# Flamingo block: side jobs of layer 1's attention reordered with two staging buffers, and layer 0's tokens scaled and shifted as rows

## The chip, the cores and the metric

The kernel runs on one core of one Trainium2 chip. The metric is the time of one execution on the device, in microseconds (us). The core has five engines that run side by side, each through its own queue in order: TensorE (PE in the profile, its weight loads PEld), VectorE (DVE), ScalarE (ACT), GpSimd (POOL) and SyncE (SP, which here issues most DMAs). They wait for each other on semaphores.

## The reference, cut to what matters

```python
x = x + tanh(g_xattn[0]) * L0_xattn(ctx_1024, layernorm(x), ...)   # 8 batches, 512 + 512 keys, 8 heads of 128
x = x + tanh(g_ffn[0])   * L0_ffn(layernorm(x))                    # 16 experts, one for each token
x = x + tanh(g_xattn[1]) * L1_xattn(layernorm(x), ctx_1024)        # 16 heads of 16
x = x + tanh(g_ffn[1])   * L1_ffn(layernorm(x))                    # 8 experts, two for each token, and a shared one

def L0_xattn(x, latents, ...):
    xn = (x - mean) * rsqrt(var + eps) * gamma_media + beta_media       # the context's 512 tokens
    ln = (latents - mean) * rsqrt(var + eps) * gamma_lat + beta_lat     # the 512 tokens of x
    q = ln @ Wq + bq ;  k, v = split(concat([xn, ln]) @ Wkv + bkv)
    return softmax(q k^T / sqrt(128)) v @ Wo + bo                       # of each head
```

All is float32. A product is made of three products in a 32-bit format of TensorE (high times high, low times high, high times low), so each operand is kept as a high part, which ScalarE rounds out of PSUM, and a low part, which VectorE makes as value minus high part.

## The kernel before, in words

**Layer 0's attention** (tiles named `a_`) goes through 64 steps, `n = 8 b + 2 hp + par`: batch `b`, and head `2 hp + par`. Below a step is written (hp, par). A step has four row tiles of scores. `plan` writes out its order by hand: `scores0..3` are the products of query and key, `turn0..3` the transposes of the probabilities (`a_probT`), `fin0/1` the two halves of the product of probabilities and values of the head before, `out0/1` that head's output projection, `qk0..2` the queries and keys of the next head, and `v0..3` the values of two heads (in steps with par 0). All that isn't scores or transposes of probabilities goes through two PSUM banks, `a_pj`, in turn: use u may start when VectorE has emptied use u-2 (`free_bank`, semaphore `pj_out`). Step (3, 1) also has `pro2 pro3 pro0 pro1`: the four transposes of the next batch's normalised tokens `a_y`. ScalarE's part of a pro applies gamma and beta by column (`a_cols`) as it writes `a_kvT_hi`; VectorE applies them to PSUM in place (L457, `TENSOR_SCALAR a_pj`), and then writes `a_kvT_lo` (L437). `a_kvT` holds two batches. PE starts `scores2` when the exponential of `scores0` is done (`exp_done`), and so on.

`normalise` (L524) makes `a_y` of tokens, mean and inverse deviation on VectorE, a `TENSOR_SCALAR` for each of 8 tiles: all 8 in the opening, and for the next batch two tiles each at two places in step (2, 1) and two in step (3, 0). GpSimd splits the weights of each head in `split_w` (L304 to L308) and computes the inverse deviations in `inverse_std` (L315 to L325).

**The opening of layer 0** loads 13 constants first (semaphore `loaded`), the two big weights into `a_prob` among them, then the tokens (`x_load`) and the first heads' weights. ScalarE and VectorE split the big weights, PE sums the values' bias (L718, 8 products), then come normalise, the four pro and three qk, and step 0.

**Layer 1's attention** (tiles named `c_`) has 64 steps too, 8 pairs of heads in 8 batches; its scores begin at L2057. Ahead of each pair a row maximum is needed (`for_maximum` on PE L2046, `maximum` on VectorE L1831, 4 for each pair, AHEAD = 4 pairs). Before step 0 the opening must do for batch 0 and batch 1: turn the context (`ctx`) and the normalised tokens (`y`), project keys and queries (`k`, `q`), values (`v`), 16 maxima, and `max 0`, their transpose. These side jobs go through two banks of `c_side`, whose turn is the list `names`. A projected k or q is written by ScalarE and VectorE (`project_high`, `project_low`) into **one** staging tile `c_stage`; SyncE's `keep` writes it to DRAM in 4 DMAs, and `set_rows` reads it back as `c_q_rows`, `c_k_rows` in four quarters. So the next project_high waits until the last keep has landed (`staged`). GpSimd's `add_experts` adds the experts' rows to x when the x loads (`x_load`, 16 for each) are in; VectorE's `measure` takes the statistics; `normalise` follows on ScalarE.

Of the kernel before, what the change touches and what calls it, by code (L numbers as in the profile page):

```python
# [10 lines left out]
ALU = mybir.AluOpType  # L11
# [45 lines left out]
def layer0_attention(nc, t_in, K, tg, route, x1_dram, tables, qk_dram):  # L57
# [11 lines left out]
    with ExitStack() as ctx:  # L69
# [11 lines left out]
        cols = sb("cols", [P, 4, DC])  # L81
# [13 lines left out]
        kvT = [sb("kvT_hi", [P, 2, DC, KV0], F32R), sb("kvT_lo", [P, 2, DC, KV0], F32R)]  # L95
# [41 lines left out]
        affine_done = sem("affine_done")  # L137
# [19 lines left out]
        PRO = (2, 3, 0, 1)  # L157

        def next_kv(b, hp, par):
            return (b + (hp == 3 and par == 1)) % 2  # L160

        def plan(b, hp, par):
# [2611 lines left out]
```

## Time and profile before

| | us |
|---|---|
| median of 3 runs (lowest to highest) | 3363.99 (3363.82 to 3366.74) |
| the profiled execution | 3363.84 |
| its span, first to last instruction | 3362.0 |
| outside the span | 1.8 |
| first scores of layer 0 | 54.34 |
| first scores of layer 1 | 1979.41 |

The profiler records one execution: for each engine every instruction's start and duration, and what ended the idle time before it. Times in its rows count from the start of the span.

### The profile page before, as it was taken

To read this page: it belongs to the slowest core of one execution; us is meant where nothing else is said; L and a number is where in the kernel's file an instruction comes from. 1 tells how busy PE (TensorE), PEld (TensorE's weight loads), DVE (VectorE), ACT (ScalarE), POOL (GpSimd) and SP (SyncE) were. 2 spreads that over 40 slices of the span, in tenths; PEclk is the share of its full clock that TensorE was granted. 3 is DMA by queue.
4 is the path that set the end of the run, shared out by engine and by line. 5 is a ranking of instruction groups with operands and counts; after the bars stand their busy time and mean duration, and the time that the engine had idled before them with its cause. 6 is when DMAs were issued, how large, how long until landed. Compare 5 with 4: busy or idle time off the path is not lost. (4 is left out here: it accounts for less than half of the span.)

```text
span 3362.0 us, 48562 instructions
## 1 busy us (share of the span) xinstructions
PE 3016.8 (90%) x18120; PEld 2452.6 (73%) x18120; DVE 2166.0 (64%) x3805; ACT 1764.1 (52%) x2738; POOL 1370.2 (41%) x1016
## 2 busy tenths in 40 slices
PE   5999999999999999999699569999999636999984
PEld 4888878888887878878599534555554636999984
DVE  5777777777777777776545467777775432666654
ACT  3554555545555545555355248888888212555541
POOL 2111111111111111111234348888877253699975
PEclk8999999999999999999899779999999567999996
DMA  7201010010001001000266343333331141477743
GB/s 236 45 10 32 10 38 10 13 35 16 29 13 35 10 16 32 10 25 4 67 205 218 110 125 118 114 114 114 114 96 39 57 160 66 136 235 232 228 148 114
DMA packets 212023, 288.41 MB, mean 86 GB/s; under 512 B 19427, under 2 KB 154754, under 8 KB 211808
## 3 DMA queue, kind: packets, MB, share of 16 engines
q1 hardware_dynamic: 201312, 256.60, 24.5%
q0 software_dynamic: 10496, 28.92, 2.5%
q8 instruction: 138, 2.26, 0.3%
q14 instruction: 77, 0.63, 0.1%
HBM read 203.86 MB, written 81.53 MB: 85 GB/s over the span
## 5 line engine op out<-in xcount | busy, mean ns | idle before, releaser
L304 POOL TENSOR_TENSOR a_w_stage<-a_w_stage,a_consts 128x256 f32<-128x256 f32 x64 | 39.3, 614 | 1230.1 <-PE a_scores L36 1205.7
L1639 POOL TENSOR_TENSOR c_pT_lo<-c_prob,c_pT_hi 128x1024 fp32r<-128x1024 f32 x192 | 456.1, 2383 | 113.4 <-ACT c_pT_hi L1721 109.5
L391 ACT ACTIVATE a_prob<-a_scores,a_neg_max 128x1024 f32<-128x1024 f32 x256 | 286.2, 1118 | 374.3 <-DVE a_neg_max L494 366.0
L494 DVE TENSOR_REDUCE a_neg_max<-a_scores 128x1 f32<-128x1024 f32 x256 | 310.3, 1212 | 108.7 <-PE a_scores L36 108.7
L384 ACT ACTIVATE a_pT_hi<-a_probT 128x512 fp32r<-128x512 f32 x512 | 278.9, 598 | 183.2 <-PE a_probT L713 183.1
L1831 DVE TENSOR_REDUCE c_neg_max<-c_max 128x2 f32<-128x1024 f32 x248 | 302.4, 1219 | 70.9 <-PE c_max L2046 70.2
L437 DVE TENSOR_TENSOR a_pT_lo<-a_probT,a_pT_hi 128x512 fp32r<-128x512 f32 x512 | 327.9, 682 | 21.2 <-ACT a_pT_hi L384 21.2
L1715 ACT ACTIVATE c_prob<-c_scores 128x1024 f32<-128x1024 f32 x256 | 261.2, 1020 | 70.8 <-PE c_scores L2057 65.7
L713 PE MATMUL a_probT<-k_ident,a_prob 128*128 128x128 f32 x2048 | 268.6, 273 | 12.1 <-DVE a_pT_lo L437 12.1
L34 PE MATMUL m_h<-m_rT_hi,m_w_hi 128*128 128x256 f32 x880 | 258.7, 294 | 17.8 <-issue 9.2
L35 PE MATMUL m_h<-m_rT_lo,m_w_hi 128*128 128x256 f32 x880 | 254.4, 289 | 13.7 <-issue 13.7
L713 PEld LDWEIGHTS a_probT<-k_ident,a_prob 128*128 128x128 f32 x2048 | 233.0, 140 | 37.9 <-issue 17.2
L36 PE MATMUL m_h<-m_rT_hi,m_w_lo 128*128 128x256 f32 x880 | 253.9, 289 | 7.0 <-issue 6.7
L2421 POOL TENSOR_TENSOR m_w_lo<-m_w_in,m_w_hi 128x1024 fp32r<-128x1024 f32 x82 | 197.0, 2403 | 134.3 <-ACT m_w_hi L2462 133.1
L2478 ACT ACTIVATE m_act_h<-m_h 128x256 f32<-128x256 f32 x220 | 84.0, 382 | 267.7 <-PE m_h L36 199.9
L34 PE MATMUL a_pj<-a_pT_hi,a_v_hi 128*128 128x512 f32 x512 | 205.5, 401 | 14.6 <-DVE a_kvT_lo L437 12.7
L1721 ACT ACTIVATE c_pT_hi<-c_prob 128x1024 fp32r<-128x1024 f32 x192 | 203.5, 1060 | 13.8
L34 PE MATMUL a_scores<-a_kT_hi,a_qT_hi 128*128 128x512 f32 x512 | 207.7, 406 | 2.3 <-DVE a_kT_lo L438 1.7
L36 PE MATMUL a_pj<-a_pT_hi,a_v_lo 128*128 128x512 f32 x512 | 205.2, 401 | 0.0
L35 PE MATMUL a_pj<-a_pT_lo,a_v_hi 128*128 128x512 f32 x512 | 204.1, 399 | 0.0
L35 PE MATMUL a_scores<-a_kT_lo,a_qT_hi 128*128 128x512 f32 x512 | 201.1, 393 | 0.0
L36 PE MATMUL a_scores<-a_kT_hi,a_qT_lo 128*128 128x512 f32 x512 | 200.9, 392 | 0.0
(335 smaller groups left out, 8720.7 us busy)
## 6 DMA issues: line engine op xcount, KB each, us to landing
m_w_in<-L_ffn_w_in SPq DMA_DIRECT2D x117, 512.0 KB
e_w_in<-L_ffn_w_in SPq DMA_DIRECT2D x32, 1024.0 KB, 7.5
qk_dram<-c_stage SPq DMA_DIRECT2D x64, 256.0 KB
c_q_rows<-qk_dram SPq DMA_DIRECT2D x32, 512.0 KB, 4.7
c_k_rows<-qk_dram SPq DMA_DIRECT2D x32, 512.0 KB, 5.7
rows_in_dram<-a_zero SPq DMA_DIRECT2D x1, 10240.0 KB, 37.6
m_row_in<-rows_in_dram SPq DMA_DIRECT2D x39, 256.0 KB
rows_out_dram<-m_res SPq DMA_DIRECT2D x39, 256.0 KB, 4.4
```

Source lines behind the costliest of these rows:

```text
L34: pe.matmul(out, l_hi, r_hi, start=start, stop=False)
L35: pe.matmul(out, l_hi, r_lo, start=False, stop=False)
L36: return pe.matmul(out, l_lo, r_hi, start=False, stop=stop)
L384: a(pT[0][:, 4 * half:4 * half + 4, qt * P:(qt + 1) * P], ps_t[:, half, :].rearrange("p (k q) -> p k q", k=4), ACT.Copy).then_inc(t_hi, 1)
L391: a(prob[:, qt, :], ps_s[:, qt % 2, :], ACT.Exp, bias=neg_max[:, qt:qt + 1], accum_out=row_sum[:, par, qt:qt + 1]).then_inc(exp_done, 1)
L437: return ve.tensor_tensor(out, ps, hi_ap.bitcast(F32), ALU.subtract)
L494: ve.tensor_reduce(neg_max[:, qt:qt + 1], ps_s[:, qt % 2, :], AX.X, ALU.max, negate=True).then_inc(max_done, 1)
L713: last = t.transpose(ps_t[:, half, k * P:(k + 1) * P], prob[:, qt, kt * P:(kt + 1) * P], ident[:])
L1639: g.tensor_tensor(flat(pT[1][:, kt - 1]), flat(prob[:, kt]), flat(pT[0][:, kt - 1]).bitcast(F32), ALU.subtract).then_inc(lo_pool, 1)
L1715: a(flat(prob[:, kt]), flat(ps_s[:]), ACT.Exp).then_inc(exp_done, 1)
L1721: a(flat(pT[0][:, kt - 1]), flat(prob[:, kt]), ACT.Copy).then_inc(hi_act, 1)
L1831: ve.tensor_reduce(two, max_bank(n, qt)[:], AX.X, ALU.max, negate=True).then_inc(max_done, 1)
```

## The change: what it does

1. Layer 0's `normalise` takes two passes of `SCALAR_TENSOR_TENSOR` over each tile: (x - mean) * gamma, then times inverse deviation plus beta. gamma and beta are held as rows, broadcast to all partitions (`a_affine`). The pro parts on ScalarE become a plain copy, and on VectorE the `TENSOR_SCALAR` on PSUM falls away. `a_kvT` holds one batch.
2. The opening of layer 0: SyncE issues the tokens and first weights ahead of the constants; GpSimd splits head 0's weights ahead of inverse_std; the big weights are split on VectorE between and after the pro and qk; VectorE waits for all 13 constants ahead of the first normalise.
3. Step (3, 1): fin0 comes behind scores2, scores3 ahead of fin1, pro0 ahead of turn0. VectorE empties pro2 and pro3 behind the next row maximum; ScalarE does an exponential at once only if scores or fin follows.
4. The opening of layer 1's attention: y and q come ahead of v, the 16 maxima are put between ctx, k and y of batch 1, and k 1 of batch 1 comes last. There are two staging tiles with a semaphore each. x 1 and x 2 are loaded late: batch 0's add_experts waits for one x load, batch 1's still for all three.

```diff
-                steps = "scores0 turn3 pro2 scores1 pro3 fin0 scores2 fin1 pro0 turn0 scores3 pro1 turn1 qk0 qk1 qk2 out0 turn2 out1"
+                steps = "scores0 turn3 pro2 scores1 pro3 scores2 fin0 scores3 fin1 pro0 turn0 pro1 turn1 qk0 qk1 qk2 out0 turn2 out1"
...
-                    last = ve.tensor_scalar(y[:, t, :], x_in[:, t, :], mv[:, t, 0:1], rstd[:, t:t + 1], ALU.subtract, ALU.mult)
+                    gamma = affine[:, 2 * (t // TB)]
+                    ve.scalar_tensor_tensor(y[:, t, :], x_in[:, t, :], mv[:, t, 0:1], gamma, ALU.subtract, ALU.mult).then_inc(scaled, 1)
+                for t in tiles:
+                    dve.wait_ge(scaled, 8 * b + (t + TB) % 8 + 1)
+                    beta = affine[:, 2 * (t // TB) + 1]
+                    ve.scalar_tensor_tensor(y[:, t, :], y[:, t, :], rstd[:, t:t + 1], beta, ALU.mult, ALU.add).then_inc(y_ready, 1)
...
+                if use == ("pro", 3):
+                    pe.wait_ge(loaded, 16 * N_CONST)
+                    bias_heads(range(0, 4))
+                elif use == ("pro", 1):
+                    bias_heads(range(4, H0)).then_inc(bias_row, 1)
...
-        stage = sb("stage", [P, 2, S], F32R)
+        stage = sb("stage", [P, 2, 2, S], F32R)
...
-                    pool.wait_ge(x_load, max(16 * b + 16, 48))
+                    pool.wait_ge(x_load, max(16 * b + 16, 48) if b else 16)
...
-                if STAGED[name]:
-                    act.wait_ge(staged, 64 * STAGED[name])
-                side_high(name, stage[:, 0])
+                number = STAGED[name]
+                if number >= 2:
+                    act.wait_ge(staged[number % 2], 64 * (number // 2))
+                side_high(name, stage[:, number % 2, 0])
```

PE's opening of layer 1 before, and now:

```diff
-            pe.wait_ge(w_lo, 5)
+            pe.wait_ge(w_lo, 4)
             project("k", 0, 0)
             project("k", 1, 0)
-            project_values(0, 0)
-            project_values(1, 0)
             turn("y", 0, 0)
             turn("y", 1, 0)
             project("q", 0, 0)
             project("q", 1, 0)
+            pe.wait_ge(w_lo, 5)
+            project_values(0, 0)
+            project_values(1, 0)
+            for qt in range(TB):
+                for_maximum(0, qt)
             turn("ctx", 0, 1)
+            for qt in range(TB):
+                for_maximum(1, qt)
+            turn_maxima(0)
             turn("ctx", 1, 1)
+            for qt in range(TB):
+                for_maximum(2, qt)
             project("k", 0, 1)
-            project("k", 1, 1)
...
+            for qt in range(TB):
+                for_maximum(3, qt)
             turn("y", 0, 1)
             turn("y", 1, 1)
+            project("k", 1, 1)
```

**VectorE in the opening of layer 0.** Before, behind the statistics (`a_var`), with the big weights' low parts (`a_wv_lo`, `a_wo_lo`) ahead of `a_y`:

```order
L519 TENSOR_SCALAR a_var<-a_mv 128x1
L539 TENSOR_TENSOR a_wv_lo<-a_prob,a_wv_hi 128x2048
L541 SCALAR_TENSOR_TENSOR a_wo_lo<-a_prob,tg,a_wo_hi 128x2048
L543 TENSOR_SCALAR a_bias<-a_bias 128x8
L545 TENSOR_TENSOR a_tbo<-a_tbo,a_probT 128x256
L547 TENSOR_SCALAR a_tbo<-a_tbo,tg 128x256
L524 TENSOR_SCALAR a_y<-a_x_in,a_mv,a_rstd 128x256 x8
L483 COPY a_qk_bias<-a_bias 128x2
L457 TENSOR_SCALAR a_pj<-a_pj,a_cols 128x512
L437 TENSOR_TENSOR a_kvT_lo<-a_pj,a_kvT_hi 128x512
```

And now, from the second half of `a_y` on:

```order
L516 SCALAR_TENSOR_TENSOR a_y<-a_x_in,a_mv,a_affine 128x256 x2
L521 SCALAR_TENSOR_TENSOR a_y<-a_y,a_rstd,a_affine 128x256 x2
L432 TENSOR_TENSOR a_kvT_lo<-a_pj,a_kvT_hi 128x512 x2
L516 SCALAR_TENSOR_TENSOR a_y<-a_x_in,a_mv,a_affine 128x256 x2
L521 SCALAR_TENSOR_TENSOR a_y<-a_y,a_rstd,a_affine 128x256 x2
L433 SCALAR_TENSOR_TENSOR a_qT_lo<-a_pj,a_qk_bias,a_qT_hi 128x512
L432 TENSOR_TENSOR a_kvT_lo<-a_pj,a_kvT_hi 128x512 x2
L544 TENSOR_TENSOR a_wv_lo<-a_prob,a_wv_hi 128x2048
L433 SCALAR_TENSOR_TENSOR a_kT_lo<-a_pj,a_qk_bias,a_kT_hi 128x512 x2
L548 SCALAR_TENSOR_TENSOR a_wo_lo<-a_prob,tg,a_wo_hi 128x2048
L550 TENSOR_TENSOR a_tbo<-a_tbo,a_probT 128x256
```

The big weights' low parts moved behind the tokens, and a_wo_lo behind the last keys, just ahead of step 0's first row maximum.

**VectorE in step (3, 1).** Before, from the first row maximum (`a_neg_max`) of the step:

```order
L494 TENSOR_REDUCE a_neg_max<-a_scores 128x1
L437 TENSOR_TENSOR a_pT_lo<-a_probT,a_pT_hi 128x4x128 x2
L457 TENSOR_SCALAR a_pj<-a_pj,a_cols 128x512
L437 TENSOR_TENSOR a_kvT_lo<-a_pj,a_kvT_hi 128x512
L494 TENSOR_REDUCE a_neg_max<-a_scores 128x1
L457 TENSOR_SCALAR a_pj<-a_pj,a_cols 128x512
L437 TENSOR_TENSOR a_kvT_lo<-a_pj,a_kvT_hi 128x512
L494 TENSOR_REDUCE a_neg_max<-a_scores 128x1
L437 TENSOR_TENSOR a_oT_lo<-a_pj,a_oT_hi 128x512
```

And now:

```order
L485 TENSOR_REDUCE a_neg_max<-a_scores 128x1
L432 TENSOR_TENSOR a_pT_lo<-a_probT,a_pT_hi 128x4x128 x2
L485 TENSOR_REDUCE a_neg_max<-a_scores 128x1
L432 TENSOR_TENSOR a_kvT_lo<-a_pj,a_kvT_hi 128x512
L485 TENSOR_REDUCE a_neg_max<-a_scores 128x1
L432 TENSOR_TENSOR a_kvT_lo<-a_pj,a_kvT_hi 128x512
L485 TENSOR_REDUCE a_neg_max<-a_scores 128x1
L432 TENSOR_TENSOR a_oT_lo<-a_pj,a_oT_hi 128x512
```

The passes over `a_pj` are gone, and each a_kvT_lo of pro2 and pro3 stands behind a row maximum.

**SyncE's queue in the opening of layer 1's attention**, from the first read back of rows on. Now (`c_stage` is the keep of q 1, `c_x` the loads of x 1 and x 2):

```order
L1559 DMA c_q_rows<-qk_dram 128x1024
L1559 DMA c_k_rows<-qk_dram 128x1024
L1548 DMA qk_dram<-c_stage 64x2x512
L1549 DMA qk_dram<-c_stage 64x512
L1548 DMA qk_dram<-c_stage 64x2x512
L1549 DMA qk_dram<-c_stage 64x512
L1537 DMA c_c_in<-ctx_in 128x4x256
L1534 DMA c_x<-x_dram 128x4x256
L1559 DMA c_q_rows<-qk_dram 128x1024
L1559 DMA c_k_rows<-qk_dram 128x1024
```

After these come the two last quarters of rows, and then x 2. Before, both x loads stood ahead of the first keep:

```order
L1556 DMA c_prob<-L_xattn_w_v_in 128x2x256
L1557 DMA c_prob<-L_xattn_w_o_in 128x2x256
L1517 DMA c_x<-x_dram 128x4x256 x2
L1530 DMA qk_dram<-c_stage 64x2x512
L1531 DMA qk_dram<-c_stage 64x512
```

So x 2 moved from ahead of all rows to behind all of batch 0's.

## Rows read from the trace of the kernel before

**Rows 1.** Windows: both openings and what follows each; PEclk 1.00 is 2.4 GHz

```profile
core 0: us, PE busy (x) PEld busy (x) DVE busy (x) ACT busy (x) POOL busy (x), PEclk, DMA share, GB/s
0.00:54.34 54.34, 17.57 (x50) 13.14 (x51) 25.29 (x46) 10.36 (x11) 13.74 (x29) 0.78 0.57 184
54.34:1650.00 1595.66, 1547.08 (x8854) 1315.44 (x8854) 1143.04 (x2059) 817.65 (x1440) 242.32 (x263) 1.00 0.09 27
1886.00:1979.40 93.40, 39.16 (x128) 25.47 (x128) 45.19 (x63) 16.41 (x32) 22.39 (x31) 0.59 0.49 152
1979.40:2560.00 580.60, 570.29 (x2807) 299.33 (x2807) 431.63 (x586) 502.07 (x609) 475.99 (x264) 1.00 0.36 107
```

**Rows 2.** Timeline of layer 0's opening: start, duration, engine, instruction, idle before it

```profile
18.72 0.20 ACT L353 ACTIVATE tg<-tg 128x4 f32<-128x4 f32 x1 [14.13 <-DMA a_prob<-L_xattn_Wo_in]
18.74 6.34 PE L718 MATMUL a_probT<-a_prob,a_bias 128*128 128x256 f32 x16 [18.74 <-DMA a_prob<-L_xattn_Wo_in]
21.32 0.89 DVE L509 BATCH_NORM_STATS2 a_stats<-a_x_in 128x6 f32<-128x256 f32 x2 [16.79 <-DMA a_x_in<-x_in]
...
25.77 3.58 POOL L315 TENSOR_TENSOR a_rstd<-a_var,a_consts 128x8 f32<-128x8 f32 x1 [22.26 <-DVE a_var L519]
27.73 2.35 DVE L541 SCALAR_TENSOR_TENSOR a_wo_lo<-a_prob,tg,a_wo_hi 128x2048 fp32r<-128x2048 f32 x1
...
32.10 6.86 DVE L524 TENSOR_SCALAR a_y<-a_x_in,a_mv,a_rstd 128x256 f32<-128x256 f32 x8 [1.23 <-POOL a_rstd L325]
...
45.62 0.80 PE L34 MATMUL a_pj<-a_kvT_hi,a_wqk_hi 128*128 128x512 f32 x1 [2.52 <-DVE a_kvT_lo L437]
...
55.99 1.23 DVE L494 TENSOR_REDUCE a_neg_max<-a_scores 128x1 f32<-128x1024 f32 x1 [1.72 <-PE a_scores L36]
```

**Rows 3.** Windows: step (3, 1) of batches 4 and 6, first scores to first scores

```profile
1020.02:1048.35 28.33, 24.91 (x128) 19.88 (x127) 19.47 (x29) 14.26 (x25) 6.93 (x7) 0.94 0.09 29
...
1423.89:1450.69 26.80, 23.38 (x128) 18.75 (x127) 19.41 (x29) 14.26 (x25) 6.93 (x7) 1.00 0.08 27
```

**Rows 4.** Timeline of PE in step (3, 1) of batch 4: three of its four waits

```profile
1026.52 0.50 PE L34 MATMUL a_pj<-a_pT_hi,a_v_hi 128*128 128x512 f32 x1 [1.80 <-DVE a_kvT_lo L437]
...
1038.95 1.16 PE L713 MATMUL a_probT<-k_ident,a_prob 128*128 128x128 f32 x8 [0.49 <-DVE a_pT_lo L437]
...
1044.30 0.51 PE L34 MATMUL a_pj<-a_kvT_hi,a_wqk_hi 128*128 128x512 f32 x1 [0.60 <-DVE a_qT_lo L438]
```

**Rows 5.** Timeline of step (3, 0), batch 4: VectorE, and PE's wait

```profile
1009.67 1.22 DVE L494 TENSOR_REDUCE a_neg_max<-a_scores 128x1 f32<-128x1024 f32 x1
...
1016.23 0.36 PE L34 MATMUL a_pj<-a_wo_hi,a_oT_hi 128*128 128x256 f32 x1 [1.16 <-DVE a_v_lo L437]
```

**Rows 6.** Timeline of layer 1's opening: the steps and waits that set it

```profile
1900.01 0.96 POOL L1623 TENSOR_TENSOR c_y<-c_y,route_w 128x256 f32<-128x256 f32 x1 [7.72 <-DMA c_x<-x_dram]
...
1927.63 0.58 SPq L1530 DMA_DIRECT2D qk_dram<-c_stage  x1
...
1932.86 0.60 ACT L1675 ACTIVATE c_stage<-c_side 128x512 fp32r<-128x512 f32 x1 [5.98 <-DMA qk_dram<-c_stage]
...
1954.03 0.60 ACT L1675 ACTIVATE c_stage<-c_side 128x512 fp32r<-128x512 f32 x1 [12.89 <-DMA qk_dram<-c_stage]
...
1955.26 1.22 DVE L1831 TENSOR_REDUCE c_neg_max<-c_max 128x2 f32<-128x1024 f32 x1
1956.39 1.22 DVE L1831 TENSOR_REDUCE c_neg_max<-c_values 128x2 f32<-128x1024 f32 x1
...
1979.41 0.79 PE L2057 MATMUL c_scores<-c_q_rows,c_k_rows 64*128 64x512 f32 x2
```

**Rows 7.** DMA issues: operation, count, KB each, median us to landing

```profile
c_q_rows<-qk_dram SPq DMA_DIRECT2D x32, 512.0 KB, 4.7
...
a_prob<-L_xattn_Wkv_in SPq DMA_DIRECT2D x1, 1024.0 KB, 6.3
```

**Rows 8.** One line's instructions: normalise on VectorE, ns min/median/max

```profile
L524 DVE TENSOR_SCALAR a_y<-a_x_in,a_mv,a_rstd x64: 402/409/1422, 32.1 to 1412.5; 128x256 f32<-128x256 f32 x64
```

More of the change, by code:

```diff
@@ L392, in exp @@
                   accum_out=row_sum[:, par, qt:qt + 1]).then_inc(exp_done, 1)
-            for i, j in enumerate(PRO):
-                use_bank(("pro", j), i, i % 2, 0, 0, 0)
-            for j in range(3):
-                use_bank(("qk", j), 4 + j, j % 2, -1, 1, 0)
+            for u, use in enumerate(FIRST):
+                use_bank(use, u, u % 2, -1, 1, 0)
             def step(b, hp, par):
@@ L402, in step @@
                 late = None
-                for kind, j in plan(b, hp, par):
-                    if kind == "scores" and j in (0, 3):
+                steps = plan(b, hp, par)
+                for (kind, j), following in zip(steps, steps[1:] + [None]):
+                    if kind == "scores" and following[0] not in ("fin", "scores"):
                         late = j
@@ L547, in _ @@
             ve.tensor_scalar(tbo[:], tbo[:], tg[:, 0:1], None, ALU.mult).then_inc(set_up, 1)
-            normalise(0, (4, 5, 6, 7, 0, 1, 2, 3))
-            set_qk_bias(0, 0)
-            for i, j in enumerate(PRO):
-                use_bank(("pro", j), i, i, i % 2, 0, 0, 0)
-            for j in range(3):
-                use_bank(("qk", j), 4 + j, 4 + j, j % 2, -1, 1, 0)
+            dve.wait_ge(set_up, 4)
             def step(b, hp, par):
@@ L714, in turn, with bias_heads @@
                     last.then_inc(t_full, 1)
-            pe.wait_ge(loaded, 16 * N_CONST)
-            for h in range(H0):
-                last = t.matmul(ps_t[:, 0, 0:D], bias[:, h, 2:3].to_broadcast([P, P]), prob[:, 2 + h // 4, h % 4 * D:(h % 4 + 1) * D], start=h == 0, stop=h == H0 - 1)
-            last.then_inc(bias_row, 1)
-            for i, j in enumerate(PRO):
-                use_bank(("pro", j), i, i % 2, 0, 0, 0, 0)
-            pe.wait_ge(pj_out, 4)
-            for j in range(3):
-                use_bank(("qk", j), 4 + j, j % 2, -1, 1, 1, 0)
+            def bias_heads(heads):
+                for h in heads:
+                    last = t.matmul(ps_t[:, 0, 0:D], bias[:, h, 2:3].to_broadcast([P, P]), prob[:, 2 + h // 4, h % 4 * D:(h % 4 + 1) * D],
+                                    start=h == 0, stop=h == H0 - 1)
+                return last
+            for u, use in enumerate(FIRST):
+                if use == ("qk", 0):
+                    pe.wait_ge(pj_out, 2)
+                elif use == ("qk", 1):
+                    pe.wait_ge(pj_out, 5)
+                use_bank(use, u, u % 2, -1, 1, 0, 0)
+                if use == ("pro", 3):
[3 more added lines that the diff above has]
+                    bias_heads(range(4, H0)).then_inc(bias_row, 1)
             def step(b, hp, par):
@@ L1811, in project_low @@
                 dve.wait_ge(x_hi, HIGH[name] + 1)
-                lo(stage[:, 1], side(name), stage[:, 0]).then_inc(x_out, 1)
+                both = stage[:, STAGED[name] % 2]
+                lo(both[:, 1], side(name), both[:, 0]).then_inc(x_out, 1)
             def value_low(i, b):
```

173 lines of the change are left out of this document (89 added, 84 removed).

## The prediction

> **What bounds the kernel now.** I read the windows first, cut where each attention's first scores start. In layer 0's main part PE is busy 1547.08 of 1595.66 us at full clock, in layer 1's 570.29 of 580.60 [rows 1]. So an edit inside these parts counts only where it takes away one of PE's few waits. The two openings are another matter: PE works 17.57 of 54.34 us and 39.16 of 93.40 us, at a granted clock of 0.78 and 0.59 [rows 1]. There a chain over all engines sets the time, and each us off it comes off the kernel. The reader is to see in the timeline of layer 0's opening that nothing starts on PE and ScalarE before the constants are in at 18.7, that the tokens are in at 21.32, that normalise starts at 32.10, behind GpSimd's inverse deviation, which starts at 25.77, and runs to the first qk at 45.62 and the first row maximum at 55.99 [rows 2]. In the main part I looked at the one step that holds the pro work. It takes 26.80 us in four of its seven batches and 28.33 in the three others [rows 3]; PE waits 3.42 us in each, the longest time 1.80, for VectorE's a_kvT_lo [rows 4]. Step (3, 0) before it has one wait, 1.16 of 1.27 us [rows 5]. In layer 1's opening the one staging tile shows as 5.98 and 12.89 us of waiting on ScalarE, behind which all 16 maxima stand [rows 6].
>
> **Layer 0, step (3, 1), seven times.** In time from the step's start, by durations of rows: PE does scores0 (1.4), turn3 (1.0), pro2 (0.5), scores1 and pro3, to 4.7. Before, fin0 needed pro2's bank, and VectorE freed it at 6.5 after row maximum, two a_pT_lo, the pass on PSUM (0.82) and a_kvT_lo (0.69): the wait of 1.80 [rows 4]. Now scores2 stands in that place. Its exponential (scores0's) ends at 4.2, so it runs from 4.6 to 6.0. VectorE does the row maximum of scores1 from 4.3 to 5.5 and a_kvT_lo to 6.1: fin0 waits 0.2. scores3 then has its exponential since 6.7 and starts at 9.0; fin1 ends at 13.2. pro0's bank was freed at 7.9. turn1 waits for the first a_pT_lo of turn0, about 0.75 (before 0.49 [rows 4]), qk2 for qk0's bank about 0.15, out1 0.1. That makes 1.2 us in place of 3.42: 2.2 x 7 = 15.4. In the three steps of 28.33 PE has the same wait and 1.53 us more busy time at a granted clock of 0.94 [rows 3]: the products behind the wait of 1.80 run for a while at the lower level. With no wait over 0.8 left I count that as gone, 3 x 1.53 = 4.6. Sum **-20.0**. Bounds: with no wait left 3.42 x 7 + 4.6 = 28.5; with a wait of 1.8 surviving and the clock falling in all seven, 1.6 x 7 - 4 x 1.53 = 5.
>
> **Layer 0, steps (2, 1) and (3, 0).** normalise doubles its instructions, 4 more in each step. The row of the present pass is 0.41 us at the median [rows 8]; two-tensor passes of that size are not in the trace, the nearest is L541, 2.35 us for 2048 columns, which by length gives about 0.3 plus a fixed part: 0.41 again. So each of the two places in a step is 0.8 us longer. In (2, 1) PE's waits are under 0.2 and VectorE idles for 2 us on either side: nothing. In (3, 0) the second place stands just ahead of the row maximum at 1009.67; scores3's exponential stands ahead of v0 on ScalarE, so a_v_lo is 0.8 later and PE's wait of 1.16 [rows 5] grows to 2.0. Batches 1 to 6 have it: **+4.8**. Bounds: 0 if VectorE's idle time takes it, 2 x 4.8 if both places reach PE. ScalarE's plain copy in place of the scaled one lies in its idle time (14.26 us busy of 28.33 [rows 3]).
>
> **Layer 0's opening.** Tokens now lead, and land near 9 to 10 by the 6.3 us of a first large load [rows 7]. Statistics and inverse deviations take as before 10.8 us (21.32 to 32.10 [rows 2]), so rstd is there near 21. The constants are then last. Tokens followed Wo by 2.6 us for 1 MB [rows 2]; ahead of the last constant stand the tokens, four rows of 128 KB in place of four small loads, and both heads' weights: 21.3 + 1 MB, 24.5. VectorE waits for them, so the first pass starts at 24.9 instead of 32.10, and the early tokens bring 7 of the 11 us that they might. From there the new chain is longer. Before: 13.5 us to the first qk, 8.7 + 1.7 more to the row maximum. Now: 12 passes (4.9, with some meeting GpSimd), pro2 and pro3, and half the bias sum (3.2, half of 6.34 [rows 2]) put qk0 at 34.1, after 9.2 us. Then three qk 7.8, pro0 and pro1 2.6, the other half 3.2, and the drain 1.5: first scores at 49.2, not 54.34. But a_wo_lo (2.35 [rows 2]) and two small steps (0.8) now stand on VectorE ahead of the row maximum: 52.6, or 52.0 as PE is at the full clock somewhat earlier. **-4.0**, from 0 (constants at 28) to -8 (constants at 21).
>
> **Layer 1's opening.** k 0 and k 1 have a tile each, so the wait of 5.98 that held k 1 and v falls away. Chain now: k at 1901.9 (two low parts of weights are behind it), both k out at 1908.7, statistics 2.4, GpSimd 1.7 and normalise 2.1, y to 1918.3, q 0 staged at 1922.7, before 1927.63 [rows 6]. Its keep lands 5.2 later (1927.63 to 1932.86), rows in 4.7 to 5.7 [rows 7]: first maximum at 1934.7, not 1955.26. The 16 maxima go at 1.13 each [rows 6]. If nothing else held them, the scores would start near 1963, a gain of 16. But batch 1's statistics stand ahead of the maxima of pair 2, and they need x 2, which SyncE now issues behind all of batch 0's rows. Before, what was issued from 1932.86 on, 6.05 MB (eight row loads of 512 KB [rows 7], two keeps of 768 KB, a context), had landed at 1954.03: 0.285 MB per us [rows 6]. Now 6.3 MB (one keep less, two x loads more) from 1928.0 on: x 2 lands at 1949 to 1950, and with the experts' rows added (5.5) the statistics end at 1955, where the maxima alone would have let them end at 1950.6. Then 8 maxima 9.0, the wait for k 0's projection and low part 2.6, y 3.3 and k 1's projection: first scores at 1970.5. **-9**, from -4 (x 2 at 1954) to -16.
>
> **Sum.** -20.0 + 4.8 - 4.0 - 9 = -28.2. The profiled execution took 3363.84, 0.15 under the median, so 3335.6 in its terms: I take **3335**.
>
> **The place where a rule and a row differ.** The passes of normalise that met GpSimd's split in the opening took 6.86 us for eight against 0.41 each elsewhere, at most 1.42 [rows 2, 8]. The new passes read two tiles. This is the third rival below. By the Trainium skill (SBUF — State Buffer, its part on the shared port pair) VectorE and GpSimd share a pair of ports, and a VectorE instruction with two SBUF inputs shuts out a GpSimd one that reads SBUF, or waits for its end. The trace agrees with it for the opening.
>
> **Rivals.** (a) *x 2 doesn't hold layer 1*: the rate of the DMAs is higher, x 2 lands by 1944, and the gain there is 16: 3328. For it speaks that rows alone land in 4.7; against it, that 6 MB took 21 us. (b) *Constants and port eat the openings*: constants at 28, x 2 at 1954; 0 and -4 there: 3363.8 - 20.0 + 4.8 - 4 = 3344.6, or 3350 where (3, 0) loses twice. (c) *The new passes are caught behind GpSimd in the main part too*: 16 passes per batch at 0.86 (6.86 / 8) are 13.8 us in place of 8 at 0.41, 3.3; if all 10.5 reached PE, 7 x 10.5 = 74 us against gains of 33 (20.0 + 4.0 + 9): 3405, slower. It decides from 33 / 7 = 4.7 us per batch on. Against it: the median of 0.41 says that nearly all passes of the main part stand clear of GpSimd's 3 us of splitting per step. (d) *The change doesn't do what it says*: the wait in (3, 1) only moves, to turn1 and qk2, and with it the lower clock; layer 1's maxima wait elsewhere: within 0.2%, 3360.
>
> **How the numbers follow.** Forecast 0.65, (a) 0.12, (b) 0.15, (d) 0.05, (c) 0.03. The range 3322 to 3350 takes in (a) and (b) and the bounds of step (3, 1). 0.2% is 6.7 us, about what a measurement of this kernel can tell from no change. Faster 0.92, same 0.05, slower 0.03.
>
> **What would show it.** PE in step (3, 1) of all seven batches in 24 to 25 us at clock 1.00, its longest wait 0.8, ahead of turn1; PE's wait in step (3, 0) 2.0; VectorE's passes at 0.41; the first pass of normalise ended by a DMA of constants near 24.5, and the first row maximum near 52; in layer 1 the first maximum near 1934.7 less what layer 0 gained, VectorE's wait for GpSimd's c_x ahead of pair 2's maxima, and 84 us from the loads to the first scores in place of 92.8. Wrong it would be if a wait in (3, 1) over 1.5 us stays, or if the constants land far from 24.5.

## The result, and the profile of the changed kernel

The changed kernel takes 3330.52 us (median of four runs, 3326.86 to 3334.41) where the kernel before takes 3363.9 (3361.78 to 3366.74): a ratio of 0.9898, with a 95% interval of 0.9886 to 0.991. The profiled execution took 3326.86 us, the lowest of the four, with a span of 3324.9; the traces therefore differ by 37.1 us of span, the medians by 33.4.

The windows of the changed kernel, cut at the same events as [rows 1] (first scores of layer 0, its last output, layer 1's first load, its first scores):

```profile
core 0: us, PE busy (x) PEld busy (x) DVE busy (x) ACT busy (x) POOL busy (x), PEclk, DMA share, GB/s
0.00:41.91 41.91, 11.35 (x50) 9.34 (x51) 20.87 (x47) 9.52 (x11) 11.57 (x29) 1.00 0.75 256
41.91:1626.20 1584.29, 1542.82 (x8854) 1312.75 (x8854) 1149.19 (x2091) 815.07 (x1440) 242.41 (x263) 1.00 0.09 27
1862.20:1948.52 86.32, 38.77 (x128) 24.96 (x128) 47.44 (x63) 16.77 (x32) 22.18 (x31) 0.58 0.50 155
```

By the starts and ends of the instructions at those events, the 37.1 us divide so:

| stretch | before | after | difference |
|---|---|---|---|
| start to layer 0's first scores | 54.34 | 41.91 | -12.4 |
| to layer 0's last instruction on PE | 1598.4 | 1587.0 | -11.4 |
| to layer 1's first load (layer 0's FFN) | 233.8 | 233.8 | 0 |
| to layer 1's first scores | 92.84 | 85.75 | -7.1 |
| to layer 1's last attention instruction on PE | 648.96 | 647.03 | -1.9 |
| the rest (gate and MoE) | 733.6 | 729.4 | -4.2 |

The last line is not the change's: below, kernels with the same code behind layer 1's attention show 733.9, 733.6, 732.3 and 729.9 us for it. The -1.9 above it isn't clear of scatter either: further kernels with the changed code for that stretch took 647.05 to 648.50 us, and a second one with the code of before 648.04.

**Layer 0's opening.** The timeline, all engines, of the stretch that answers to [rows 2]:

```profile
17.04 0.20 POOL L322 TENSOR_TENSOR a_rstd<-a_rstd,a_vtmp 128x4 f32<-128x4 f32 x1
...
22.40 0.17 DVE L533 TENSOR_SCALAR a_bias<-a_bias 128x8 f32<-128x8 f32 x1 [9.11 <-DMA r_wg<-L_ffn_Wg_in]
...
23.49 2.68 DVE L516 SCALAR_TENSOR_TENSOR a_y<-a_x_in,a_mv,a_affine 128x256 f32<-128x256 f32 x4
...
29.57 2.63 PE L729 MATMUL a_probT<-a_prob,a_bias 128*128 128x256 f32 x8
32.27 0.39 PE L35 MATMUL a_pj<-a_kvT_lo,a_wqk_hi 128*128 128x512 f32 x1
32.50 0.39 PE L36 MATMUL a_pj<-a_kvT_hi,a_wqk_lo 128*128 128x512 f32 x1
...
41.91 0.50 PE L34 MATMUL a_scores<-a_kT_hi,a_qT_hi 128*128 128x512 f32 x1 [1.56 <-DVE a_kT_lo L433]
...
45.67 1.21 DVE L485 TENSOR_REDUCE a_neg_max<-a_scores 128x1 f32<-128x1024 f32 x1
```

The inverse deviations are ready at 17.2 us (they were ready at 32), but VectorE stands still from 13.3 us on, 9.11 us in all, until the last of the thirteen constants has landed at 22.4. The other thing to see is the step from 32.27 to 32.50: a product of 512 columns every 0.23 us, which is TensorE's 2.4 GHz. Before the change the same two products of qk 0 stood 0.43 us apart, and the granted clock from 45 to 51 us was 0.50, which is 1.2 GHz:

```profile
46.21 0.63 PE L35 MATMUL a_pj<-a_kvT_lo,a_wqk_hi 128*128 128x512 f32 x1
46.64 0.63 PE L36 MATMUL a_pj<-a_kvT_hi,a_wqk_lo 128*128 128x512 f32 x1
```

**Layer 0's steps.** Windows of steps (2, 1), (3, 0) and (3, 1) in batch 4; the last answers to [rows 3]:

```profile
952.96:975.20 22.24, 21.39 (x117) 17.56 (x115) 16.85 (x30) 11.52 (x21) 2.94 (x3) 1.00 0.04 13
975.20:1003.87 28.67, 26.66 (x161) 23.09 (x159) 23.05 (x53) 13.47 (x24) 2.95 (x3) 1.00 0.04 10
1003.87:1028.18 24.31, 23.23 (x128) 18.70 (x127) 16.21 (x25) 13.91 (x25) 6.92 (x7) 1.00 0.10 33
```

PE's waits in the same three steps, in order of time (two in (3, 1), which answer to [rows 4]; two in (3, 0), which answer to [rows 5]; one in (2, 1)):

```profile
973.22 1.16 PE L724 MATMUL a_probT<-k_ident,a_prob 128*128 128x128 f32 x8 [0.85 <-DVE a_pT_lo L432]
...
995.44 0.39 PE L34 MATMUL a_pj<-a_wv_hi,a_kvT_hi 128*128 128x256 f32 x1 [0.77 <-DVE a_kT_lo L433]
1000.07 0.36 PE L34 MATMUL a_pj<-a_wo_hi,a_oT_hi 128*128 128x256 f32 x1 [1.14 <-DVE a_v_lo L432]
...
1019.97 1.16 PE L724 MATMUL a_probT<-k_ident,a_prob 128*128 128x128 f32 x8 [0.63 <-DVE a_pT_lo L432]
1024.13 0.50 PE L34 MATMUL a_pj<-a_kvT_hi,a_wqk_hi 128*128 128x512 f32 x1 [0.27 <-DVE a_qT_lo L433]
```

Step (3, 1) takes 24.3 us in all seven batches, for 26.80 or 28.33: its total is 22.1 us less. Step (3, 0) takes 28.68 in batches 1 to 6 for 27.81, and step (2, 1) 22.24 for 21.42; with 26.98 for 26.28 and 22.01 for 21.11 in batch 0 that is 5.9 and 5.8 us back. The two passes of normalise take 0.48 us each, not 0.41 [rows 8]; this is one of them, by the view of one line's instructions (ns min/median/max):

```profile
L516 DVE SCALAR_TENSOR_TENSOR a_y<-a_x_in,a_mv,a_affine x64: 472/477/1490, 23.5 to 1390.5; 128x256 f32<-128x256 f32 x64
```

**Layer 1's opening.** The timeline of the stretch that answers to [rows 6]; the first load is issued at 1862.77:

```profile
1912.62 1.23 DVE L1851 TENSOR_REDUCE c_neg_max<-c_max 128x2 f32<-128x1024 f32 x1 [4.74 <-PE c_max L2067]
1915.95 0.45 SPq L1534 DMA_DIRECT2D c_x<-x_dram  x1
1926.32 0.61 POOL L1641 TENSOR_TENSOR c_y<-c_y,route_w 128x256 f32<-128x256 f32 x1 [26.89 <-DMA c_x<-x_dram]
1927.76 0.43 DVE L1883 BATCH_NORM_STATS2 c_stats<-c_x 128x6 f32<-128x256 f32 x1 [1.64 <-POOL c_x L1643]
...
1932.63 1.22 DVE L1851 TENSOR_REDUCE c_neg_max<-c_max 128x2 f32<-128x1024 f32 x1
```

The first maximum comes 49.8 us after the first load's issue (before 68.7), and then x 2, issued at 1915.95 and landed at 1926.24, holds GpSimd, GpSimd holds the statistics, and the statistics hold the maxima of pair 2 until 1932.63.

### The profile page after: what moved, and what is told of

Same layout as the page of the kernel before. It is cut to its first block and busy times, and to the rows that moved or that the text cites. A ratio compares the mean times of both kernels' runs of the same rounds, so it can differ in the third digit from the quotient of the medians.

```text
span 3324.9 us, 48629 instructions
## 1 busy us (share of the span) xinstructions
PE 3004.4 (90%) x18120; PEld 2444.0 (74%) x18120; DVE 2167.5 (65%) x3837; ACT 1761.1 (53%) x2738; POOL 1368.5 (41%) x1016
```

## The experiments

Each is an edit of the changed kernel where nothing else is said. All but the last were executed once. Four of them (the undone order, the passes at another place, the one staging buffer, the early token loads) ran beside the kernel before at 3368.86 us; with the traces above they make up the first group. The other seven, the second group, ran later, beside the kernel before at 3280.83 or 3282.35 us: in them the gate and MoE take some 80 us less, 649.3 to 651.9 us for 729.4 to 733.9. The record doesn't put this down to the chip: it gives the first four and the last three to run the same chip number. What the traces show is that in the first group ScalarE waits in the MoE, at the activation that makes `m_act_h`, for what the profile calls "remote" (68.2 us in the changed kernel, 34.7 to 72.4 in the six traces), and never in the second group; the cause is open.

So I compare stages, and whole times only within a group. The steps of layer 0 agree in both groups to some 0.05 us. Three other stages scatter between kernels with the same code for them: the stretch up to the first scores by 1.3 us (41.91 to 43.16), layer 1's opening by 1.1 (85.11 to 86.22), and its main part by 1.5 (647.03 to 648.50).

### The order in step (3, 1), undone

```diff
-  steps = "scores0 turn3 pro2 scores1 pro3 scores2 fin0 scores3 fin1 pro0 turn0 pro1 turn1 qk0 ...
+  steps = "scores0 turn3 pro2 scores1 pro3 fin0 scores2 fin1 pro0 turn0 scores3 pro1 turn1 qk0 ...
-  if kind == "scores" and following[0] not in ("fin", "scores"):
+  if kind == "scores" and j in (0, 3):
-  if kind == "pro" and j > 1:
+  if False:
```

> Layer 0's step (3,1) with its old order of side jobs, and ScalarE's and VectorE's rules on which side job is held back as they were; the scale and shift pass on the accumulator stays removed. Theory: the order and the removed pass each take a part of the 3.4 us that TensorE stood in this step: the step takes 25.3 to 27 us in place of 24.30, so 7 to 19 us over the seven. Rival: the removed pass alone did it, and the step stays at 24.3 within 0.3 us. In both, steps (2,1) and (3,0) stay at 22.24 and 28.68.

The step takes 24.77 to 24.79 us in all seven batches, with steps (2, 1) and (3, 0) unchanged at 22.24 and 28.68. The window and PE's two waits of the step in batch 5:

```profile
1206.95:1231.74 24.79, 22.71 (x128) 18.85 (x127) 16.02 (x25) 13.43 (x25) 6.92 (x7) 1.00 0.09 31
```
```profile
1212.40 0.49 PE L34 MATMUL a_pj<-a_pT_hi,a_v_hi 128*128 128x512 f32 x1 [0.79 <-DVE a_kvT_lo L432]
1227.71 0.49 PE L34 MATMUL a_pj<-a_kvT_hi,a_wqk_hi 128*128 128x512 f32 x1 [1.28 <-DVE a_qT_lo L433]
```

Neither theory has the number, but the rival is nearer. The pass on PSUM that the change removed was worth 2.0 us a step (26.80 to 24.78) and all three drops of the clock; the order on top of it 0.48 us a step, 3.4 us in all. Of the 22.1 us, 18.7 are the removed pass, together with ScalarE's plain copy and the smaller `a_kvT`, which this kernel keeps and no run takes apart. The wait of 1.80 that I read as a matter of order [rows 4] is down to 0.79 in the old order, since the pass of 0.82 us no longer stands ahead of a_kvT_lo on VectorE. All of PE's waits in the step fall from 3.42 to 2.08 us, although the one for a_qT_lo grows from 0.60 to 1.28. Batch 0's first step takes 21.50 us here for 20.33, another 1.2 us once; where it is lost stays open.

### One pass of normalise

```diff
-  ve.scalar_tensor_tensor(y[:, t, :], x_in[:, t, :], mv[:, t, 0:1], gamma, ...).then_inc(scaled, 1)
-  for t in tiles:
-      dve.wait_ge(scaled, 8 * b + (t + TB) % 8 + 1)
-      ve.scalar_tensor_tensor(y[:, t, :], y[:, t, :], rstd[:, t:t + 1], beta, ...).then_inc(y_ready, 1)
+  ve.scalar_tensor_tensor(y[:, t, :], x_in[:, t, :], mv[:, t, 0:1], gamma, ...).then_inc(y_ready, 1)
```

> This kernel leaves out the second pass of the normalising (the inverse deviation and the shift are not applied), and leaves the first where the change has it, behind the first turn. Theory: the second pass of each tile, two in step (2,1) and two in step (3,0), is what these steps lost against the kernel before: they go back to its 21.42 and 27.81, about 10 us less over six batches. Rival: the place alone decides, and any pass at that place costs the whole of what moving them gave back: the steps stay at 22.24 and 28.68 within 0.15. Second rival: even one pass is hidden there, and the steps take 21.36 and 27.10, as where the passes were moved behind scores 2.

The kernel leaves out the inverse deviation and the shift. Steps (2, 1) and (3, 0) take 21.44 and 27.88 us in batches 1 to 6, as the first theory has it; the other steps stay. So the second passes, four in each of the two steps, cost 0.80 us a step. In (2, 1) most of it is the wait ahead of turn 2, which is 0.30 us here and 0.85 us with two passes:

```profile
964.64 1.16 PE L719 MATMUL a_probT<-k_ident,a_prob 128*128 128x128 f32 x8 [0.30 <-DVE a_pT_lo L432]
```

### The same passes at another place

```diff
+  elif after == ("scores", 2):            # behind the maximum of scores 2
+      if at == (2, 1) and ahead:
+          normalise(b + 1, (6, 7))
+      elif at == (3, 0) and ahead:
+          normalise(b + 1, (2, 3))
```
(and these two calls taken out behind the first turn; each step's other two tiles stay behind scores 1)

> VectorE's normalising of tiles 6, 7 and of 2, 3 (two passes a tile now) is moved in steps (2,1) and (3,0) from behind the first turn to behind the third block of scores' maximum. Theory: the doubled passes cost there because they stand ahead of a low half that TensorE waits for; behind scores 2 they lie where VectorE has slack, and the steps go back to 21.4 to 21.6 and 27.8 to 28.1, 7 to 11 us over the seven batches together. Rival: VectorE has no slack anywhere in these two steps, and they stay at 22.24 and 28.68 within 0.15 wherever the passes stand. Second rival: the passes now hold the last maximum and TensorE waits longer, 22.5 and 29 or more.

Steps (2, 1) and (3, 0) take 21.36 and 27.10 us, with both passes of each tile in them; step (3, 1) stays at 24.30. Layer 0's first scores to last instruction fall from 1587.0 to 1570.5 us, 16.5 less. The windows of the two steps in batch 4, and the only wait of PE in (3, 0), where there were two:

```profile
944.88:966.25 21.37, 21.16 (x117) 17.64 (x116) 16.94 (x30) 11.42 (x21) 2.94 (x3) 1.00 0.05 13
966.25:993.32 27.07, 26.12 (x160) 23.00 (x159) 23.11 (x53) 13.57 (x24) 2.95 (x3) 1.00 0.04 11
```
```profile
989.53 0.35 PE L34 MATMUL a_pj<-a_wo_hi,a_oT_hi 128*128 128x256 f32 x1 [0.95 <-DVE a_v_lo L432]
```

VectorE does as much as before (16.94 and 23.11 us for 16.85 and 23.05 at the old place), and PE waits 1.7 us less in the two steps (0.85 and 2.01 us before, 0.21 and 0.95 now). Why is to be seen on VectorE in step (2, 1), first of the changed kernel, then of this one:

```profile
965.78 0.69 DVE L432 TENSOR_TENSOR a_oT_lo<-a_pj,a_oT_hi 128x512 fp32r<-128x512 f32 x1 [2.21 <-ACT a_oT_hi L374]
...
967.82 0.87 DVE L516 SCALAR_TENSOR_TENSOR a_y<-a_x_in,a_mv,a_affine 128x256 f32<-128x256 f32 x2
968.61 0.88 DVE L521 SCALAR_TENSOR_TENSOR a_y<-a_y,a_rstd,a_affine 128x256 f32<-128x256 f32 x2
969.40 1.22 DVE L485 TENSOR_REDUCE a_neg_max<-a_scores 128x1 f32<-128x1024 f32 x1
```
```profile
955.42 0.87 DVE L516 SCALAR_TENSOR_TENSOR a_y<-a_x_in,a_mv,a_affine 128x256 f32<-128x256 f32 x2
956.21 0.88 DVE L521 SCALAR_TENSOR_TENSOR a_y<-a_y,a_rstd,a_affine 128x256 f32<-128x256 f32 x2
957.71 0.69 DVE L432 TENSOR_TENSOR a_oT_lo<-a_pj,a_oT_hi 128x512 fp32r<-128x512 f32 x1 [0.62 <-ACT a_oT_hi L374]
...
959.75 1.22 DVE L485 TENSOR_REDUCE a_neg_max<-a_scores 128x1 f32<-128x1024 f32 x1
```

In the changed kernel VectorE stands idle for 2.21 us, and only then come the passes, right ahead of the maximum of scores 3, on which ScalarE's exponential and all behind it hang. A few instructions earlier the same four passes lie in that idle time (0.62 us of it is left), and the maximum of scores 3 starts 14.9 us after the step's start, not 16.4 (959.75 - 944.88 and 969.40 - 952.96). The first theory holds, and the gain is half as large again as leaving the second passes out gives (16.5 us of layer 0's main part for 11.2), which leaves room for the single pass at the old place to cost something too.

### The place, in the kernel before

The same move, made in the kernel before, whose normalise has one pass of 0.41 us.

> The kernel before with its single pass of normalising in steps (2,1) and (3,0) moved behind scores 2, like the moved double passes. Theory: the place, not the number of passes, is what these steps pay for once the passes have slack: they take 21.36 and 27.1 instead of 21.42 and 27.81, so 4 to 5 us over six batches, and step (3,1) stays at 26.8 or 28.3. Rival: only the doubled passes were in the way, and the steps stay at 21.42 and 27.81.

Step (3, 0) takes 27.15 us for 27.81, step (2, 1) 21.42 as before. So one pass reached PE in (3, 0) and was hidden in (2, 1): the theory holds for one step of the two. But layer 0's main part gains only 1.0 us (1597.4 for 1598.4) of the 4, because step (3, 1) now takes 28.32 us in five batches of seven, where it did in three. Batches 0 and 5:

```profile
216.67:244.99 28.32, 24.87 (x129) 19.86 (x128) 19.46 (x29) 14.26 (x25) 2.94 (x3) 0.94 0.04 10
1223.02:1249.81 26.79, 23.34 (x128) 18.74 (x127) 19.40 (x29) 14.27 (x25) 6.92 (x7) 1.00 0.09 29
```

The same instructions and the same 3.4 us of waiting go with 1.53 us more of busy time where the granted clock is 0.94, and which batches have it changed with 0.66 us less in the step before; what decides it stays open.

### The bias sum behind the projections

```diff
-  if use == ("pro", 3):
-      bias_heads(range(0, 4))
-  elif use == ("pro", 1):
-      bias_heads(range(4, H0)).then_inc(bias_row, 1)
+  if use == ("qk", 2):
+      bias_heads(range(0, H0)).then_inc(bias_row, 1)
```

> All eight products of the bias sum stand behind qk 2 in TensorE's opening, in place of four behind pro 3 and four behind pro 1. Theory: these products (2.63 and 1.89 us on TensorE) raised its granted clock to full before the projections qk, and without them the projections run at the lower level, with matmuls of 0.43 us apart in place of 0.235: 18 matmuls of each of three projections cost some 3 to 8 us more, and the first scores come no earlier than with them, at 41.9 or later. Rival: the products only lengthen TensorE's chain: without them ahead the first scores come at 37.5 to 39.5.

The 3.9 us of products (2.28 and 1.58 by the starts) now stand between the projections and the first scores, and these come 3.6 us later, at 45.48. PE's timeline, two products of projection qk 0, the bias sum and the first scores:

```profile
31.72 0.63 PE L35 MATMUL a_pj<-a_kvT_lo,a_wqk_hi 128*128 128x512 f32 x1
32.15 0.63 PE L36 MATMUL a_pj<-a_kvT_hi,a_wqk_lo 128*128 128x512 f32 x1
...
42.21 3.62 PE L729 MATMUL a_probT<-a_prob,a_bias 128*128 128x256 f32 x16
45.48 0.58 PE L34 MATMUL a_scores<-a_kT_hi,a_qT_hi 128*128 128x512 f32 x1
```

Most of the projections' products are 0.43 us apart, 1.2 GHz, where they are 0.23 apart in the changed kernel. Their last one starts at 41.98 us for 39.96, 2.0 us later, with 3.9 us less of work ahead of it: in the changed kernel the bias halves filled two waits for a_kvT_lo, of 1.41 us each here. So the clock theory holds, and the lengthening one is out. The other 1.6 of the 3.6 us are not the clock's: the bias sum runs from 42.21 to 45.48, where the changed kernel waits 1.56 us for a_kT_lo. By batch 1's start 2.3 us of the 3.6 remain (232.74 for 230.41). The granted clock in the windows shows it late: 1.00 from 28 to 36 us, in which the products already go at 0.43, and 0.79 from 36 to 44.

### The constants that are needed first, first

```diff
-  dma(prob[:, 0:2, :], wv_v).then_inc(loaded, 16)         # now behind the affine rows and biases
-  dma(prob[:, 2:4, :]..., wo_v).then_inc(loaded, 16)
-      dma(affine[:, i], ...).then_inc(loaded, 16)          # the three biases likewise
+      dma(affine[:, i], ...).then_inc(early, 16)
-  dve.wait_ge(loaded, 16 * N_CONST)
+  dve.wait_ge(early, 16 * 7)
```
(ScalarE splits the two big weights behind its second and fifth bank; the first half of the bias sum stands behind qk 0)

> The four affine rows and the three bias columns are loaded ahead of the value and output weights and counted on a semaphore of their own, so VectorE's first normalising waits for seven loads in place of thirteen; ScalarE splits the two big weights behind the banks that use_bank takes second and fifth, and TensorE's first half of the bias sum comes behind qk 0. Theory: the 9.11 us that VectorE waited for the last constant held the whole opening: the first maximum of a row comes at 40 to 42 us instead of 45.7. Rival: another chain is as long (the inverse deviations, ready at 17.2, then 8 tiles of two passes, transposes and projections), and the first maximum comes no earlier than 44.5. Second rival: the big weights' later arrival or their splits hold the first output of layer 0 up, and the first batch gives back what the opening wins.

The first scores come at 36.97 and the first maximum at 40.73, 4.9 us earlier, and the first transposes at 20.49 in place of 27.81. The first theory holds, and so does the second rival, by half: batch 0's step (1, 0) takes 29.32 us for 26.72, and batch 1 starts only 2.4 us earlier. The longest wait in this step (GpSimd's split for its weights, us in total, times, longest), and SyncE's queue ahead of it:

```profile
POOL a_w_stage L302 <- DMA a_w_stage<-L_xattn_Wkv_in: 29.6, 1, 29.6
```
```profile
81.38 1.56 SPq L261 DMA_DIRECT2D qk_dram<-k_ones  x1
...
85.86 0.51 SPq L229 DMA_DIRECT2D a_w_stage<-L_xattn_Wq_in  x1
```

PE waits 1.7 us in one piece for the a_kT_lo behind that split. The weight pair's load stands behind the DMAs that clear scratch memory, and these keep the queue until 83 us however early the work on the engines begins.

### The same, with the loads ahead of the small clears

```diff
+  def load_early():
+      sp.wait_ge(acc_init, 1)
+      load_tokens(1)
+      sp.wait_ge(w_split, 3)
+      load_w(4, 4, 0)
+      sp.wait_ge(w_split, 4)
+      load_w(5, 5, 1)
+  load_early()        # behind the two big clears, ahead of the sixteen small ones
```

> The kernel with the constants first, and the loads of the second batch's tokens and of the weight pairs 4 and 5 moved on SyncE's queue ahead of the sixteen small DMAs that clear qk_dram (the two big clears stay ahead). Theory: those clears kept the queue until 83 us, so that weight pair 4 landed at 91.6 and batch 0's step (1,0) had TensorE wait 2.41 us for it: the step goes back from 29.32 to 26.7, and batch 1 starts at about 225.5 instead of 228.0. Rival: the big clears of 14 MB, which land until 67 us, or another wait hold this step: it stays above 28.

Step (1, 0) of batch 0 takes 26.73 us, and batch 1 starts at 225.76, 4.65 us earlier than in the changed kernel. The loads now go out at 58.45 to 65.3, and GpSimd's split waits for PE alone. The theory holds.

### One staging buffer

```diff
-  side = STAGED[kind, c, b] % 2
+  side = 0
-  if number >= 2:
-      act.wait_ge(staged[number % 2], 64 * (number // 2))
+  if number:
+      act.wait_ge(staged[0], 64 * number)
```

> Layer 1 with the new order of side jobs, but with a single staging buffer, as before the change. Theory: the second buffer matters, since k1, q0 and q1 of the opening each wait for the DMAs that empty the buffer (about 2 to 2.5 us each on ScalarE): the stretch from the first context load to the first scores grows from 85.8 by 4 to 8 us, and layer 1's main part (647.0) stays within 1 us. Rival: the new order alone made the gain, and the stretch grows by at most 1 us.

From the first load's issue to the first scores 90.11 us pass, 4.4 more. Layer 1's main part takes 648.55 for 647.03, no more than its scatter. ScalarE's timeline, the high part of q 1, which waits as k 1's does (6.05):

```profile
1910.80 0.60 ACT L1691 ACTIVATE c_stage<-c_side 128x512 fp32r<-128x512 f32 x1 [5.97 <-DMA qk_dram<-c_stage]
```

The theory holds: of the 7.1 us of layer 1's opening the second buffer brings 4.4, the order alone some 2.7, with 1 us of scatter on either. What the buffer does for the main part is not shown.

### The token loads of batches 1 and 2 early

```diff
+  load_x(1)
+  load_x(2)
   keep("k", 0, 0)
...
-  load_x(1)            # where the change has them
-  load_x(2)
```
(x 0 counts on a semaphore of its own)

> Layer 1's loads of x 1 and x 2 are issued again ahead of the first keep, as before the change (x 0 counts on a semaphore of its own). Theory: x 2, issued at 1915.95 behind the rows and landed at 1926.24, holds VectorE's measure(1) and so the maxima: the last batch of maxima comes some 2.5 to 4 us earlier, and the stretch from the first context load's issue to the first scores goes from 85.8 to 82 to 83.5 us. Rival: the maxima of pairs 2 and 3 wait for ScalarE and TensorE anyway, and the stretch stays at 85.8 within 0.5. Second rival: the loads ahead of keep hold the rows up by the 3 to 6 us that such a load takes, the first maximum moves from 1912.6 to 1915 or later, and the stretch grows to 87 to 89.

The stretch takes 80.76 us, 5.0 less. VectorE's timeline, the statistics and the first maximum of pair 2, 65.0 us after the first load's issue for 69.9:

```profile
1925.92 0.42 DVE L1884 BATCH_NORM_STATS2 c_stats<-c_x 128x6 f32<-128x256 f32 x1
...
1928.25 1.22 DVE L1852 TENSOR_REDUCE c_neg_max<-c_max 128x2 f32<-128x1024 f32 x1
```

Here they start as soon as the low parts ahead of them are done. The first theory holds, and the gain goes beyond its range (82 to 83.5). The whole kernel took as long as the changed one (3326.8), because the gate and MoE, which it leaves alone, took 4.5 us longer in this execution and the first scores came 1.2 later; that is why I don't judge a stage by the kernel's time.

### Layer 1's part alone

The kernel before, with `layer1_attention` of the changed one.

> The kernel before, with layer 1's attention as after. Theory: the two parts of the change add up: layer 0's stages are those of the kernel before (first maximum 56.0, step (3,1) 26.8 or 28.3), and the stretch from layer 1's first context load to its first scores is 85.8 within 0.5, its main part 647.0: the time is 9 us below the kernel before. Rival: the stretch depends on how layer 0 left the chip (clock, queues), and is 88 or more.

The stretch takes 85.11 us, the main part 647.05, layer 0 is that of the kernel before (step (3, 1) 26.8 or 28.3). The time is 3269.35 us beside 3280.83. The parts add up: layer 1's opening is as long as behind the changed layer 0, within its scatter.

### All of them together

The moved normalise, the constants first, the loads ahead of the small clears, and x 1 and x 2 early.

> All four edits together: the normalising behind scores 2, the constants first, the token and weight loads ahead of the small clears, and layer 1's x 1 and x 2 loaded with x 0. Theory: the gains add up, since each lies in a stage of its own: minus 14.8 (steps (2,1) and (3,0)), minus 4.9 (first maximum 40.7, with batch 0's step (1,0) at 26.7), minus 5.0 (layer 1's opening at 80.8): 24 to 25 us below the changed kernel and 58 below the kernel before on the same chip. Rival: the earlier weight pair and the moved passes bring out waits elsewhere, and it is less than 18 us below the changed kernel.

It takes 3222.02 us (median of five, 3220.42 to 3223.89) beside 3282.35 of the kernel before (nine runs of the same group): a ratio of 0.9821, interval 0.9807 to 0.9834, 60 us less. The windows, cut as the first ones above:

```profile
0.00:36.71 36.71, 13.22 (x51) 10.44 (x51) 20.55 (x47) 9.52 (x11) 11.45 (x29) 1.00 0.70 226
36.71:1604.30 1567.59, 1537.40 (x8854) 1312.83 (x8854) 1150.64 (x2091) 814.84 (x1440) 242.58 (x263) 1.00 0.10 29
1840.71:1921.44 80.73, 39.56 (x128) 25.74 (x128) 46.75 (x63) 16.75 (x32) 22.70 (x31) 0.58 0.54 166
```

The gains add: 5.2 us in the opening, 16.7 in layer 0's main part, 5.0 in layer 1's opening against the changed kernel. The changed kernel itself was not timed in this group; by its ratio of 0.9898 it would stand near 3249 there, an estimate.

## Why the prediction was right, and where its steps were off

I predicted 3335 in a range of 3322 to 3350; it is 3330.5. Step by step:

- **Step (3, 1), -20.0.** Measured -22.1: 24.3 us at clock 1.00 in every batch, longest wait 0.63 ahead of turn 1. Right in size and in signature; PE waits 1.08 us in a step, for which I said 1.2. The cause was half wrong: I followed the new order through the step and gave it the whole gain, but the undone order shows 18.7 of the 22.1 us without it: the removed pass frees each bank 0.82 us sooner, and the drops of the clock go with it.
- **Step (3, 0), +4.8.** Measured +5.9, of which the second pass explains 0.80 us a step by the one-pass kernel. My mechanism was off: a_v_lo's wait did not grow (1.14 for 1.16), but a new one of 0.77, for a_kT_lo, joined it.
- **Step (2, 1), nothing.** This is the term that failed: +5.8. I took PE's waits of under 0.2 and VectorE's 2 us of idle time on either side as cover. The idle time was there (2.21 us), but it ends before the passes start, and they stood ahead of the maximum of scores 3. The moved passes show that both are true at once: the same work, a few instructions earlier, costs nothing. The price of a pass was low as well: I took 0.41 us and wrote that passes of that size with two tiles are not in the trace, but they are, 256 of the same operation at 0.48 us (the row of L469 at the end), which is what the new ones take. By that row the eight passes in a step are 0.6 us dearer than I had them.
- **Layer 0's opening, -4.0 (first maximum 52.0).** Measured -10.3 (45.67), and -12.4 at the first scores. The wait for the constants was the right one, and ended 2.1 us sooner than I put it (22.4, not 24.5). From the first pass to the first scores I counted 24.3 us; it was 18.4. The missing 5.9 is the clock: I priced qk at 7.8 us and the bias halves at 6.4, by rows of the kernel before, which ran that stretch at the lower level; by their starts they took 4.5 and 3.9. The kernel with the bias sum last shows the lower level come back when PE has less to do between its waits. This term lay outside its own bounds (0 to -8).
- **Layer 1's opening, -9.** Measured -7.1. The first maximum came 49.8 us after the first load (forecast 48.1), x 2 landed after 63.5 (forecast 63 to 64), and the stretch took 85.75 for 84. The early loads confirm the cause: without the wait for x 2 it is 5.0 us less.
- **Not forecast:** -1.0 in layer 0's other steps, none of which moved by more than 0.2 us, and the -1.9 and -4.2 of layer 1's main part and the gate and MoE, about as much as these two scatter between kernels with the same code.

In sum the forecast terms came to -28.2, and the same stages measured -22.1 + 5.9 + 5.8 - 12.4 - 7.1 = -29.9: an error of 6 in one place (step (2, 1)) and of 8 in another (the opening) cancelled. That the sum came within 2 us is luck; the terms of step (3, 1), step (3, 0) and layer 1's opening came within 2.1 us each on their own. Rival (a) is out, as x 2 did hold layer 1; (b) is out, as the constants landed at 22.4. Rival (c) is out: of the 128 new passes one took 1.49 us, in the opening, from 23.88 to 25.37 beside GpSimd's split from 23.63 to 25.10, and the 127 others took 0.47 to 0.48. By the Trainium skill (SBUF — State Buffer, "Who interferes with whom") a VectorE instruction with two inputs in SBUF contends with a GpSimd one that reads SBUF, and the one that was issued second waits for the first. The trace agrees in this one pass, which ended 0.27 us behind the split; no run here takes it apart. The slow passes of the kernel before (up to 1.42 us [rows 8]) had one tile in, so they are no test of what the rule says of two inputs. (d) is out by step (3, 1).

## What to carry to other kernels

Idle time of an engine covers added work only where that work stands ahead of the idle time in the engine's own order: before calling it free, find the next result of the engine that others wait for, and see that the idle time lies between the two. When a pass is removed and an order is changed in one go, price the removed pass at every bank it frees before the order gets the credit. When an opening is shortened, read what else stands on its queue (here clearing DMAs, until 83 us), since that is the next wall, and don't price TensorE's work there by rows at the level at which it ran before.

## What the runs showed of the hardware that I had not expected

- TensorE's level in the opening hung on what was put between its waits. With half of the bias sum (8 matmuls, 2.28 us) ahead of qk 0 and half (1.58 us) ahead of qk 1, the projections' products were 0.23 us apart, without them mostly 0.43, and the projections ended 2.0 us later with 3.9 us less of work ahead of them. The granted clock in the windows showed the lower level only later (1.00 from 28 to 36 us, 0.79 from 36 to 44).
- The price of a VectorE pass went by its operation here, not by the number of its tiles. For 128x256 a `SCALAR_TENSOR_TENSOR` with two tiles in takes 0.48 us, a `TENSOR_TENSOR` with two tiles in 0.42, and normalise's `TENSOR_SCALAR` with one 0.41 [rows 8]. The first line is of the kernel before (ns min/median/max), the second of the changed one (us in all, then the mean in ns):

```profile
L469 DVE SCALAR_TENSOR_TENSOR x_acc<-a_pj,a_inv_sum,x_acc x256: 474/476/485, 94.7 to 1653.3; 128x256 f32<-128x256 f32 x128
```
```profile
L2551 DVE TENSOR_TENSOR m_hT_lo<-m_g,m_hT_hi 128x256 fp32r<-128x256 f32 x64 | 26.9, 421 | 3.0 <-ACT m_hT_hi L2508 0.8
```

- The gate and MoE, the same code throughout, took 729.4 to 733.9 us in six executions, and 649.3 to 651.9 in the seven later ones, three of them under the same chip number as four of the first, while the steps of layer 0 agreed to some 0.05 us. Times of whole kernels from different groups say nothing here; stages do.
